# Graph attention in two layers: the softmax probabilities are split into fp16 halves before the transposes instead of behind them

## The reference

```
h = max(layernorm(x), 0)
q, k, v = h @ Wq + bq, h @ Wk + bk, h @ Wv + bv      # 6 heads of 64
probs = softmax(q k^T / 8 + (0 where adj, else -9e15))
x = x + (probs @ v) @ Wf + bf
```

## Time and profile before

| | |
|---|---|
| median of three runs | 2118.2 us (2116.44 to 2121.31) |
| the profiled execution | 2120.55 us, its span 2118.6 us |
| PE busy | 2023.7 us, 96% of the span |
| DVE busy | 1753.7 us, 83% |
| POOL busy | 1338.2 us, 63% |
| ACT busy | 1266.0 us, 60% |
| granted TensorE clock, mean | 0.984 of full speed |

### The profile page before, as it was taken

How to read it: one execution, slowest core, us unless ns; L and a number is a source line. 1 busy time by engine, 2 the same in 40 slices (tenths; PEclk the granted TensorE clock), 3 DMA queues, 4 the chain that set the end, 5 groups by cost and what they waited for, 6 DMA issues and landing times.

```text
span 2118.6 us, 62046 instructions
## 1 busy us (share of the span) xinstructions
PE 2023.7 (96%) x18832; PEld 1220.1 (58%) x18832; DVE 1753.7 (83%) x6074; ACT 1266.0 (60%) x2249; POOL 1338.2 (63%) x1810
## 2 busy tenths in 40 slices
PE   1689999999999999999999999999999999999996
PEld 0356666666566566656665666666566665666653
DVE  4488888888888888888888888888888888888875
ACT  2266666666666566666666666666666666666652
POOL 3366666666666666666666666666666666666652
PEclk7899999999999999999999999999999999999998
DMA  5433444444444444444544444444444444444433
GB/s 155 124 85 105 111 116 135 134 133 117 127 132 135 130 131 121 129 129 131 137 134 124 115 132 129 136 131 136 115 131 131 136 134 135 130 115 117 115 94 94
DMA packets 443713, 264.91 MB, mean 125 GB/s; under 512 B 341987, under 2 KB 443365, under 8 KB 443365
## 3 DMA queue, kind: packets, MB, share of 16 engines
q1 hardware_dynamic: 443364, 260.76, 44.5%
HBM read 134.75 MB, written 125.83 MB: 123 GB/s over the span
## 4 chain that ended last, share of the span: by engine, by line
PE 45%; issue 24%; POOL 21%; DMA 4%; DVE 3%; SPq 2%; ACT 1%; POOLq 1%; DVEq 0%; ACTq 0%
PE ps_proj L467 8%; PE ps_proj L469 8%; PE ps_proj L468 8%; POOL x_tile L402 5%; POOL ht_lo L418 5%; PE ps_pt L510 5%; POOL ct_lo L406 5%; PE ps_out L467 4%; PE ps_out L468 4%; PE ps_out L469 4%; PE ps_scores L541 4%; POOL rstd L391 3%; DMA c_moved<-c_dram 3%; POOL probs L411 2%; POOL shift L393 1%
## 5 line engine op out<-in xcount | busy, mean ns | idle before, releaser
L411 POOL TENSOR_TENSOR probs<-probs,row_max 128x768 f32<-128x768 f32 x256 | 376.0, 1469 | 586.7 <-DVE row_max L822 586.7
L643 ACT ACTIVATE probs<-probs,exp_scale 128x768 f32<-128x768 f32 x256 | 239.7, 936 | 257.9 <-POOL probs L411 257.9
L800 DVE SCALAR_TENSOR_TENSOR qk_lo<-ps_proj,qk_bias,qk_hi 128x512 f16<-128x512 f32 x384 | 282.8, 737 | 130.8 <-ACT qk_hi L630 130.8
L822 DVE CUSTOM_DVE_ANT_0 probs<-ps_scores,mask 128x128 f32<-128x128 f32 x1536 | 342.4, 285 | 0.7 <-PE ps_scores L541 0.5
L599 ACT ACTIVATE pt_hi<-ps_pt 128x384 f16<-128x384 f32 x512 | 223.0, 487 | 151.1 <-PE ps_pt L510 150.9
L467 PE MATMUL ps_proj<-wv_hi,ht_hi 128*128 128x384 f16 x768 | 252.8, 329 | 43.4 <-DVE wv_lo L739 24.6
L630 ACT ACTIVATE qk_hi<-ps_proj,qk_bias 128x512 f16<-128x512 f32 x384 | 258.7, 674 | 31.5 <-PE ps_proj L469 31.4
L467 PE MATMUL ps_out<-wf_hi,ct_hi 128*128 128x384 f16 x768 | 251.8, 328 | 19.6 <-DVE ctx_n L812 12.4
L785 DVE TENSOR_TENSOR pt_lo<-ps_pt,pt_hi 128x384 f16<-128x384 f32 x512 | 260.3, 550 | 0.2 <-ACT pt_hi L599 0.2
L406 POOL TENSOR_TENSOR ct_lo<-c_moved,ct_hi 128x384 f16<-128x384 f32 x256 | 233.9, 914 | 37.3 <-ACT ct_hi L638 37.0
L402 POOL TENSOR_TENSOR x_tile<-x_tile,out_bias 128x384 f32<-128x384 f32 x256 | 255.9, 1000 | 1.9 <-DVE out_bias L745 1.9
(11 more groups left out here) (91 smaller groups left out, 5000.6 us busy)
## 6 DMA issues: line engine op xcount, KB each, us to landing
h_dram<-h_blocks SPq DMA_DIRECT2D x256, 192.0 KB, 1.9
h_moved<-h_dram SPq DMA_DIRECT2D x1024, 48.0 KB, 1.9
c_dram<-c_blocks SPq DMA_DIRECT2D x256, 192.0 KB, 1.9
c_moved<-c_dram SPq DMA_DIRECT2D x1024, 48.0 KB, 2.0
x_tile<-in_x SPq DMA_DIRECT2D x32, 768.0 KB, 5.3
out_x<-x_tile SPq DMA_DIRECT2D x128, 192.0 KB, 1.9
adj_u<-in_adj SPq DMA_DIRECT2D x64, 64.0 KB, 2.1
wq_raw<-in_L_gnn_Wq SPq DMA_DIRECT2D x2, 576.0 KB, 6.4
```

Source lines behind the costliest of these rows:

```text
L411: nc.gpsimd.tensor_tensor(probs[i % 2][:, :, :], probs[i % 2][:, :, :], row_max[i % 2][:, :].rearrange("p (a o) -> p a o", o=1) .to_broadc ...
L800: nc.vector.scalar_tensor_tensor(out=qk_lo[b][:, chunk, :], in0=ps_proj[bank_of("qk", chunk)][:, :], scalar=qk_bias[layer_of(t)][:, chunk ...
L822: ins = nc.vector.tensor_tensor_reduce(probs[i % 2][:, s, :], ps_scores[s // PAIRS][:, (s % PAIRS) * P:(s % PAIRS + 1) * P], mask[b][:, i, ...
```

## The change

The exponential now stays in SBUF and is split there: ACT writes its fp16 high half `p_hi` (one instruction of 768 elements, straight behind the exponential), POOL writes `p_lo` = probs - `p_hi` in the next slot (768 elements). TensorE then transposes twelve fp16 blocks, six of `p_hi` into one PSUM bank and six of `p_lo` into the other, both banks now holding fp16. ACT copies the first bank to `pt_hi` and DVE the second to `pt_lo`, each in one instruction of 768 elements. `p_hi`, `p_lo`, `pt_hi` and `pt_lo` have one buffer each. TensorE's transposes move behind the q/k pieces of the slot, and the copies out of PSUM open the next slot on ACT and DVE. The core of the diff:

```diff
@@ POOL
+            def probs_lo(t, i, m):
+                wait(pool, pt_turned, unit_count(t, m, 2 * PER, 2 * i))
+                pool.wait_ge(p_hi_set, unit_count(t, m, PER, i + 1))
+                nc.gpsimd.tensor_tensor(p_lo[:, :, :], probs[i % 2][:, :, :], p_hi[:, :, :], ALU.subtract
+                                        ).then_inc(p_split, 1)
...
                     if exists(nu):
                         norm(nu, ni, m)
+                    if exists(pu):
+                        probs_lo(pu, pi, m)
@@ TensorE
-                wait(pe, pt_set, unit_count(t, m, 2 * PER, 2 * i))
-                pe.wait_ge(exp_done, unit_count(t, m, PER, i + 1))
-                for s in range(HEADS):
-                    mm = pe.transpose(ps_pt[s // PAIRS][:, (s % PAIRS) * P:(s % PAIRS + 1) * P],
-                                      probs[i % 2][:, s, :], ident[:, :])
-                    if s % PAIRS == PAIRS - 1:
-                        mm.then_inc(pt_turned, 1)
+                wait(pe, pt_hi_set, unit_count(t, m, PER, i))
+                wait(pe, pt_lo_set, unit_count(t, m, PER, i))
+                pe.wait_ge(p_split, unit_count(t, m, PER, i + 1))
+                for turned, half in ((ps_pt[0], p_hi), (ps_pt[1], p_lo)):
+                    for s in range(HEADS):
+                        mm = pe.transpose(turned[:, s * P:(s + 1) * P], half[:, s, :], ident16[:, :])
+                    mm.then_inc(pt_turned, 1)
@@ ACT
+                wait(act, pt_turned, unit_count(t, m, 2 * PER, 2 * i))
+                act.wait_ge(exp_done, unit_count(t, m, PER, i + 1))
+                nc.scalar.activation(p_hi[:, :, :], probs[i % 2][:, :, :], ACT.Copy).then_inc(p_hi_set, 1)
+
+            def turned_hi_out(t, i, m):
+
+                wait(act, ctx_summed, unit_count(t, m, PER, i))
+                act.wait_ge(pt_turned, unit_count(t, m, 2 * PER, 2 * i + 1))
+                nc.scalar.activation(pt_hi[:, :, :], ps_pt[0][:, 0:HEADS * P].rearrange("p (a k) -> p a k", a=HEADS),
+                                     ACT.Copy).then_inc(pt_hi_set, 1)
...
                     if exists(t):
                         exp(t, i, m)
+                        probs_hi(t, i, m)
@@ DVE
-            def probs_lo(t, i, m):
-                for s in range(2):
-                    dve.wait_ge(pt_hi_set, unit_count(t, m, 2 * PER, 2 * i + 1 + s))
-                    nc.vector.tensor_tensor(pt_lo[i % 2][:, s * PAIRS:(s + 1) * PAIRS, :],
...
+            def turned_lo_out(t, i, m):
+
+                wait(dve, ctx_summed, unit_count(t, m, PER, i))
+                dve.wait_ge(pt_turned, unit_count(t, m, 2 * PER, 2 * i + 2))
+                nc.vector.tensor_copy(pt_lo[:, :, :], ps_pt[1][:, 0:HEADS * P].rearrange("p (a k) -> p a k", a=HEADS)
+                                      ).then_inc(pt_lo_set, 1)
...
+                    if exists(cu):
+                        turned_lo_out(cu, ci, m)
```

More of the change, by code:

```diff
@@ L158, in build @@
         ident = sb("ident", [P, P], F32)
+        ident16 = sb("ident16", [P, P], F16)
         minus_half = sb("minus_half", [P, 1], F32)
@@ L200, in build @@
         row_max = [sb(f"row_max{k}", [P, HEADS], F32) for k in range(2)]
-        pt_hi = [sb(f"pt_hi{k}", [P, HEADS, NODES], F16) for k in range(2)]
-        pt_lo = [sb(f"pt_lo{k}", [P, HEADS, NODES], F16) for k in range(2)]
+        p_hi = sb("p_hi", [P, HEADS, NODES], F16)
+        p_lo = sb("p_lo", [P, HEADS, NODES], F16)
+        pt_hi = sb("pt_hi", [P, HEADS, NODES], F16)
+        pt_lo = sb("pt_lo", [P, HEADS, NODES], F16)
         row_rcp = sb("row_rcp", [P, HEADS], F32)
@@ L208, in build @@
         ps_scores = [bank("ps_scores0"), bank("ps_scores1")]
-        ps_pt = [bank("ps_pt0"), bank("ps_pt1")]
+        ps_pt = [ctx.enter_context(nc.psum_tensor(f"ps_pt{s}", [P, 1024], F16)) for s in range(2)]
+        ps_bias = [ps_pt[l][:, 0:2 * H].bitcast(F32) for l in range(LAYERS)]
         ps_out = bank("ps_out")
@@ L249, in build @@
         exp_done = sem("exp_done")
+        p_hi_set = sem("p_hi_set")
+        p_split = sem("p_split")
         pt_turned = sem("pt_turned")
         pt_hi_set = sem("pt_hi_set")
-        pt_set = sem("pt_set")
+        pt_lo_set = sem("pt_lo_set")
         ctx_summed = sem("ctx_summed")
@@ L429, in slot @@
                         setup(1)
+                    pu, pi = graph_at(t, i, -1)
                     if exists(nu):
                         norm(nu, ni, m)
+                    if exists(pu):
+                        probs_lo(pu, pi, m)
                     if exists(t + 1):
@@ L450, in _ @@
                                     base=0, pattern=[[-1, P]], channel_multiplier=1).then_inc(ident_set, 1)
+            pool.wait_ge(ident_set, 1)
+            nc.gpsimd.tensor_copy(ident16[:, :], ident[:, :]).then_inc(ident_set, 1)
             slot(FIRST, None)
@@ L460, in setup @@
                 pe.wait_ge(f_loaded, 16 * (l + 1))
-                acc = ps_pt[l][:, 0:H]
+                acc = ps_bias[l]
                 for c in range(KT):
@@ L522, in apply_probs @@
                     wait(pe, ctx_ready, unit_count(t, m, PER, i))
-                pe.wait_ge(pt_set, unit_count(t, m, 2 * PER, 2 * i + 2))
+                pe.wait_ge(pt_hi_set, unit_count(t, m, PER, i + 1))
+                pe.wait_ge(pt_lo_set, unit_count(t, m, PER, i + 1))
                 for s in range(HEADS):
                     hd = head_of(s)
-                    mm = three(ps_out[:, hd * VW:(hd + 1) * VW], pt_hi[i % 2][:, s, :], pt_lo[i % 2][:, s, :],
+                    mm = three(ps_out[:, hd * VW:(hd + 1) * VW], pt_hi[:, s, :], pt_lo[:, s, :],
                                v_hi[b][:, i, hd, :], v_lo[b][:, i, hd, :])
@@ L567, in slot @@
                         score(t, i, m)
-                    if exists(tu):
-                        turn_probs(tu, ti, m)
                     if exists(pu):
@@ L576, in slot @@
                             project_qk(t + 1, piece, m)
+                    if exists(tu):
+                        turn_probs(tu, ti, m)
                     if exists(ou):
                         output(ou, oi, m)
-            pe.wait_ge(ident_set, 1)
+            pe.wait_ge(ident_set, 2)
             slot(FIRST, None)
@@ L593, in probs_hi @@
             def probs_hi(t, i, m):
-                vu, vi = graph_at(t, i, -2)
-                wait(act, ctx_summed, unit_count(vu, m, PER, vi + 1))
-                for s in range(2):
[L598 to L601, removed]
+                wait(act, pt_turned, unit_count(t, m, 2 * PER, 2 * i))
[6 more added lines that the diff above has]
+                                     ACT.Copy).then_inc(pt_hi_set, 1)
             def relu(t, i, m):
@@ L655, in slot @@
                     nu, ni = graph_at(t, i, 10)
-                    pu, pi = graph_at(t, i, -1)
+                    pu, pi = graph_at(t, i, -2)
                     hu, hi = graph_at(t, i, 8)
+                    if exists(pu):
+                        turned_hi_out(pu, pi, m)
                     if exists(cu):
@@ L665, in slot @@
                         v_hi_out(t + 1, i, m)
-                    if exists(pu):
-                        probs_hi(pu, pi, m)
                     if exists(hu):
@@ L744, in keep_out_bias @@
                 dve.wait_ge(out_bias_summed, l + 1)
-                nc.vector.tensor_copy(out_bias[l][:, :], ps_pt[l][:, 0:H]).then_inc(out_bias_set, 1)
+                nc.vector.tensor_copy(out_bias[l][:, :], ps_bias[l]).then_inc(out_bias_set, 1)
             def statistics(t, i, m):
@@ L856, in slot @@
                         mask_and_max(t, i, m)
-                    if exists(pu):
-                        probs_lo(pu, pi, m)
                     if exists(cu):
```

5 lines of the change are left out of this document (removed).

## The result

The changed kernel takes 2354.48 us (median of four runs, 2352.32 to 2358.44) against 2118.33 us before; the ratio is 1.1115, 95% interval 1.1096 to 1.1135. It is 11% slower. The forecast was 2327 us, with a range of 2300 to 2440.

What follows compares the result with a forecast made beforehand. A ring of DVE, POOL and ACT was to become the bound: 7.35 + 0.84 + 0.47 = 8.66 us a slot against 7.838. Over 244 slots 200.6 us, with start and end 208.5, so about 2327 us, range 2300 to 2440.

Steps and rivals of the forecast that it cites:

- The old ring of 7.35 us with 0.49 of slack: DVE, POOL and ACT wait in a circle needing 7.35 us a slot, 0.49 under the 7.838 that TensorE sets.
- `p_hi` costs 0.84: On ACT, between exponential and q/k chunk, the new instruction lengthens the ring by 0.84 us a slot, bounds 0.67 and 0.94.
- The copy costs 0.47 (by bytes) and not 0.87 (by elements): On DVE, between `qk_lo` and the transpose of h, the copy to `pt_lo` adds 0.47 us a slot to the ring.
- Rival 1: DVE's copy goes by elements: ring 9.06 us, 100 us more, 2427 us; chance 0.26.
- DVE's removed subtractions are worth nothing: Two subtractions leave DVE behind the mask, outside the ring; their time becomes more waiting before `qk_lo`, gain nothing.
- `p_lo` is hidden on POOL: POOL's new subtraction, 1.7 us, fits its idle time before the next maximum subtraction; 7.2 us of work, under the ring.
- Rival 3: POOL becomes the bound if `p_lo` doubles to 3.5 us: slot 9.0 us, 2410 us; chance 0.05.
- TensorE's twelve blocks enter at nothing: The fp16 turn changes TensorE's slot by 0.05 us less, at worst 0.6 more, under the ring, so nothing in the sum.
- Rival 2: TensorE's turn is slow and ACT's `p_hi` waits for it: about 60 us more, 2390 us; chance 0.07.
- The product with V waits for the residual sum: TensorE's product with V waits for DVE's residual sum of the same slot, where the ring reaches TensorE; near 0.8 us.
- Start and end, 8 us: Outside the 244 slots: start 2.6 and about 2 us more, end 1.3 and 2 for the last graph's longer way.

Runs made afterwards that it cites:

- experiment 5: Kernel before, with ACT also writing an fp16 copy of the probabilities, which nobody reads, straight behind the exponential: 2224.98 us, ratio 1.0505.
- experiment 2: Changed kernel with `p_hi` written on ACT behind the slot's q/k chunk instead of between exponential and chunk: 2146.44 us, ratio 1.0139 to the kernel before.
- experiment 3: Changed kernel with DVE's copy to `pt_lo` moved ahead of the last q/k chunk's low half, in the slot of the turn: 2250.42 us, ratio 1.0629.
- experiment 4: Changed kernel with DVE making the copy of the turned low half twice, first into a tile nobody reads: 2467.11 us, ratio 1.1666.
- experiment 1: Changed kernel with POOL computing `p_lo` for 32 elements of one head alone, the other low halves staying zero: 2353.17 us, ratio 1.1114.
- experiment 7: experiment 6 with TensorE's turn after the first two q/k pieces and ACT's copy to `pt_hi` ahead of its wait for the exponential: 2116.65 us, ratio 0.9997.
- experiment 6: Changed kernel with the moves of experiment 2 and experiment 3 together: 2124.88 us, ratio 1.0041 to the kernel before.

## Why the prediction was right, point by point

- *The old ring of 7.35 us with 0.49 of slack.* Right; experiment 5 shows it in the kernel before (8.263 measured, 8.28 added up). In the kernel before itself eleven slots from graph 7 to 251 are 7.35 or 7.36 long, and just one is shorter (7.25).
- *`p_hi` costs 0.84.* Mechanism right, size too small. The ring took 1.03 + 0.74 - 0.84 = 0.93 more. The instruction itself is short, 0.74 to its follower; but it reads what the exponential has just written, waits for that on its own engine, and so starts 1.03 after it, where an instruction that does not depend on it starts after 0.84. In experiment 2 the step from exponential to chunk is 0.84 again. The 0.09, over 244 slots 22 us, are the mis-sized term. The forecast was 27 us low; the rest is small and of both signs: the mean slot, with the loop's turns and the longer single slots, is 0.03 above what the 0.09 explain (6 us more), start and end cost 5 less than I had, and the median lies 2 above the profiled time where it had lain 2 below (4.5 more).
- *The copy costs 0.47 (by bytes) and not 0.87 (by elements).* Right: 0.46, duration 0.55 for 768 fp16 elements, the duration of the f32 copy of 384 elements. Rival 1 is out. The Trainium skill, VectorE: DVE Perf Modes, section "Why PSUM operands drop a tier", allows a PSUM operand two elements a cycle in 16 bits and one in f32. The trace agrees: twice the elements took the same 0.55 us. Experiments 3 and 4 priced the copy in both directions, 104 us less and 113 more; 115 and 117 had been added up.
- *DVE's removed subtractions are worth nothing.* Right: DVE lost 148 us of work, and its wait ahead of `qk_lo` grew from 130.8 to 600.6 us.
- *`p_lo` is hidden on POOL.* Right: 1.64 us (1.7 said), and experiment 1 gives 0. Rival 3 is out.
- *TensorE's twelve blocks enter at nothing.* Right for the sum: 0.05 less a slot said, 0.04 measured (0.67 for 0.71). But 0.80 for the old turn was too much, since 0.09 of it is the change-over behind the scores, and that stays (experiment 7). The forecasts of experiments 6 and 7, which took 0.13 off TensorE's slot, rested on it; this is one reason why no version that makes the whole computation came out faster. Rival 2 is out: ACT waited for the turn ahead of `p_hi` for 3.0 us in all.
- *The product with V waits for the residual sum.* Right: 186.6 us, 231 times, 0.8 a slot.
- *Start and end, 8 us.* Measured: graph 7's subtraction comes 5.4 us later, the stretch behind graph 251 is 47.8 long instead of 50.3. 3 us instead of 8; the end did not get longer. The last four slots have no q/k chunk, and took 25.0 us instead of 23.7; the stretch behind the last subtraction is 22.8 instead of 26.6, and why it got shorter is open.

## What to carry to other kernels

When several in-order engines hand work round in each iteration, write down the ring: follow who releases whom until you are back at the first engine, and compare its length, by starts, with the bound engine's iteration. Once the ring is the bound, a new instruction costs its full length if it stands in the ring, even right behind a wait of its own engine; before that, only what goes beyond the ring's slack. It costs next to nothing outside the path: ahead of the wait, as the copy in experiment 3, or behind the instruction that hands the ring on, as `p_hi` in experiment 2. Then look for the next ring through the same engine (experiment 6). Only the order tells these apart, the busy share doesn't; and before paying for a cheaper operation on the bound engine, measure what of the old one's time is the change-over around it.

## What the runs showed of the hardware

- DVE copies 768 fp16 elements from PSUM to fp16 in SBUF in 0.55 us (0.46 to the next start), the time of 384 f32 elements. ACT gains nothing of the kind: its copy of the same size out of PSUM takes 0.80 us, 0.69 to the next start, against 0.49 for 384 f32 elements (`v_hi`).
- Two instructions of ACT of which the second reads the first's result start 1.03 apart, where the exponential and a follower that does not read its result start 0.84 apart; the profile shows this 0.1 (1018.17 + 0.94 = 1019.11 to 1019.20) as no idle time with a releaser.
- Turning a 128 x 128 block costs TensorE 0.056 us in fp16 (0.67 / 12) and 0.118 in f32 (0.71 / 6), so a pair of fp16 halves costs what one f32 block does.
